# The scan of the source ranking reads its ones from PSUM in place of SBUF

## The reference, cut to what matters

```
edge_index = jnp.stack([src, dst])
...
sums = jnp.zeros((n_entities, res.shape[-1]), res.dtype).at[head].add(res)
counts = jnp.zeros((n_entities,), res.dtype).at[head].add(1.0)
return sums / jnp.clip(counts, 1.0, None)[:, None]
```

## Time and profile before

| | us |
|---|---|
| median of 3 runs | 19270.44 |
| lowest, highest | 19254.84, 19276.73 |
| the profiled execution, timed | 19271.95 |
| its span in the profile | 19270.1 |
| scatter's loop in it: first call to the end of the last call | 542.3 to 2855.0 |
| of it, blocks with `order_node`: first scan to last scan | 1574.3 to 2802.3 |

### The profile page before, as it was taken

The page is one execution under the profiler, slowest core; times in us unless marked ns, Lnnn a source line. Parts: engine busy times, 40 slices in busy tenths (PEclk is TensorE's granted clock), DMA queues, the critical chain, the costliest instruction groups (busy, mean ns, idle before and its releaser), DMA issues. The chain is left out here.

```text
span 19270.1 us, 218526 instructions
## 1 busy us (share of the span) xinstructions
PE 9310.3 (48%) x50893; PEld 6358.9 (33%) x50894; DVE 14747.2 (77%) x25325; ACT 3949.6 (20%) x9903; POOL 12260.2 (64%) x12680
## 2 busy tenths in 40 slices
PE   0343325566666666655777763333243334344343
PEld 0333322232233233222333353333243334334333
DVE  8556668999999999998888832221488888688887
ACT  0111101111111111111000000000144444344443
POOL 0677876666666666663777727777376665566663
PEclk9999996666666666666888855555555655565555
DMA  5333221111111111112222211112532223233223
GB/s 212 76 83 72 69 71 29 25 27 26 25 27 26 25 26 27 25 25 24 29 30 29 28 13 26 26 26 26 66 75 70 73 74 62 69 75 75 68 73 55
DMA packets 1107684, 958.58 MB, mean 50 GB/s; under 512 B 758507, under 2 KB 874859, under 8 KB 1097292
## 3 DMA queue, kind: packets, MB, share of 16 engines
q0 software_dynamic: 368704, 436.55, 12.9%
q1 hardware_dynamic: 738316, 514.36, 10.4%
HBM read 736.74 MB, written 212.93 MB: 49 GB/s over the span
## 5 line engine op out<-in xcount | busy, mean ns | idle before, releaser
L1585 POOL DMA_INDIRECT tail<-ball,h_idx x3328 | 3493.3, 1050 | 2040.4 <-issue 1005.9
L835 PE MATMUL p_rad<-w_stack,hid_t 99*128 99x512 bf16 (+1 forms) x6656 | 2659.1, 551 | 2397.0 <-DVEq L932 1331.9
L905 DVE TENSOR_REDUCE red<-prod 128x96 f32<-128x1536 f32 x1664 | 2901.0, 1743 | 3.5
L1616 PE MATMUL h_sum<-head,h_hot 128*128 128x64 f32 x6656 | 1248.5, 375 | 3164.2 <-ACT head L1671 2993.5
L1616 PEld LDWEIGHTS h_sum<-head,h_hot 128*128 128x128 f32 x6656 | 1220.1, 287 | 3177.0 <-issue 3177.0
L343 POOL DMA_INDIRECT rec_a<-rec,slot x1600 | 1825.3, 1141 | 516.5 <-issue 487.2
L1229 POOL DMA_INDIRECT l_xg<-h_tab,l_idx x1664 | 1570.0, 944 | 835.9 <-issue 500.5
L835 PEld LDWEIGHTS p_rad<-w_stack,hid_t 99*128 99x128 bf16 (+1 forms) x6656 | 716.3, 122 | 4024.7 <-issue 3894.3
L1028 POOL DMA_INDIRECT l_xg<-x_tab,l_idx x1664 | 1570.2, 944 | 658.6 <-issue 493.3
L1042 PE MATMUL l_sum<-outer,l_hot 128*128 128x512 f32 x3328 | 1664.5, 665 | 531.2 <-DVEq L1087 531.2
L752 POOL DMA_INDIRECT l_xg<-in_x,l_idx x1664 | 1577.7, 948 | 522.9 <-issue 475.4
(11 more groups left out here) (408 smaller groups left out, 19410.8 us busy)
## 6 DMA issues: line engine op xcount, KB each, us to landing
hot_t<-rows_l SPq DMA_DIRECT2D x208, 512.0 KB
rec_a<-fill SPq DMA_DIRECT2D x128, 728.0 KB, 19.4
l_rec<-rec_a SPq DMA_DIRECT2D x104, 896.0 KB, 4.8
rhot_t<-rows_r SPq DMA_DIRECT2D x208, 384.0 KB
tail<-ball,h_idx POOLq DMA_INDIRECT x3328, 2.5
t<-in_type SPq DMA_DIRECT2D x100, 512.0 KB
l_xg<-in_x,l_idx POOLq DMA_INDIRECT x1664, 2.4
l_xg<-x_tab,l_idx POOLq DMA_INDIRECT x1664
```

The source lines that it names most:

```text
L835: ins = pe.matmul(p_rad[j % 3][:, h * 512:(h + 1) * 512], hid_t[j // 4 % 2][0:K3 + 3 * (1 - i), j % 4, i, :], w_stack[i][0:K3 + 3 * (1 - i ...
L905: ch.step(dve.tensor_reduce(red[q][:, j, :], prod[j % 3][:, :, :], AX, ALU.add))
L1585: pool.indirect_dma_start(tg[q][:, j, :], None, table[:, :], bass.IndirectOffsetOnAxis(ap=idx[q][:, j:j + 1], axis=0)).then_inc(gathered[q ...
L1616: ins = pe.matmul(p_sum[u % 2][:, j % BT // 2, :], hot[j // HP8 % 3][:, j % HP8, :], hg[:, j, 0:D], start=(j % 2 == 0), stop=(j % 2 == 1))
```

## The change

The first tensor of the scan in `order_node` is `p_row[0:EP, 1:2]`, the column of PSUM that holds 1.0, broadcast to 1600 elements, where it was the SBUF tensor. The result is the same. The scan in `rank_phase` keeps the SBUF tensor, and the tensor stays allocated and filled. No instruction is added, removed or moved on any engine.

```
             def order_node(c):
                 ch.do(dve.tensor_scalar(mask[:, :], high[:, :], g["row"][0:EP, bass.ds(c, 1)], None, ALU.is_equal))
-                ch.do(dve.tensor_tensor_scan(run[:, :], g["ones_et"][:, :], mask[:, :], offs[:, bass.ds(c, 1)], ALU.mult, ALU.add))
+                ch.do(dve.tensor_tensor_scan(run[:, :], p_row[0:EP, 1:2].broadcast_to([EP, ET]), mask[:, :], offs[:, bass.ds(c, 1)], ALU.mult, ALU.add))
                 ch.do(dve.copy_predicated(order[:, :], mask[:, :].bitcast(U32), run[:, :]))
```

## The result

The changed kernel takes 19135.92 us (median of 6 runs, 19124.11 to 19146.55), the kernel before 19260.89 (6 runs, 19254.84 to 19276.73): 125 us less, a ratio of 0.9934 with a 95% interval of 0.9921 to 0.9947. The prediction was 19161, between 19133 and 19208.

What follows compares the result with a forecast made beforehand. GpSimd's calls were taken to pace the blocks that rank by source. Gains of 63.8 us (q = 0) and 45.6 us (q = 1) made 109, so 19270.4 - 109 = 19161 us, range 19133 to 19208.

Steps and rivals of the forecast that it cites:

- What bounds the blocks: In the blocks that rank by source, GpSimd's calls set the pace; VectorE has 7.3 us to spare in each block.
- Kinds of inputs: A GpSimd call starting under a VectorE instruction with two SBUF tensors waits for its end; with one in PSUM it doesn't.
- The first rival: At the source ranking's scan: it holds GpSimd calls as before, whatever its inputs; no change, 19270 us; chance 0.08.
- The scan's own time: The source ranking's scan stays at 3.55 us, 0.02 shorter to 0.1 longer, hidden under VectorE's waiting; worth nothing by itself.
- The walk, q = 0: GpSimd calls at the scan in 25 blocks with q = 0: four done instead of two, 2.55 us each, 63.8 us.
- The walk, q = 1: GpSimd calls at the scan in 24 blocks with q = 1: gain 1.27 or 2.55 us, mean 1.9 taken, 45.6 us.
- the upper bound: Far end of the saving: two GpSimd calls gained in each of 49 source-ranking blocks, 49 × 2.55 = 125 us.
- The first block: First of 50 source-ranking blocks: no gain, since its scan comes behind `place_nodes`, when VectorE is late and isn't waiting.
- The copy: Predicated copy behind the scan takes back part of the gain: with q = 0 it costs a call 1.33 us, before 0.82.

## Why the prediction was right

*What bounds the blocks.* GpSimd's calls, as it said. To do the scan from PSUM twice cost 21 to 33 us of some 180, and to leave it out gained nothing (the calls add 4 us); a second scan from SBUF, which holds a call, cost 106 to 110.

*Kinds of inputs.* The step from three other operations to the scan held: 125 calls start inside the 50 scans of the changed kernel, and the longest of them is like any undisturbed one, 0.97 us. The same broadcast from SBUF freed no call. The first rival, a scan that holds whatever it reads, is out by the result itself.

*The scan's own time.* 3.549 us against 3.551, no change. The fixed part that the Trainium skill ("VectorE: DVE Perf Modes", section on the TRN2 errata) gives a PSUM source, 62 cycles more, isn't seen: the scan is not longer by 0.065 us. That rule gave a sum of 125 us, which is near the result, but not for its reason.

*The walk, q = 0.* Four calls where there were two, as walked through: the calls start 0.30, 1.57, 2.85 and 4.12 us behind the scan's start, and the walk had them at 0.30, 1.58, 2.85 and 4.12.

*The walk, q = 1.* This is the term that was mis-sized. I took 24 × 1.9 = 45.6 us as the mean of one call gained and two; the call starts 0.01 us before the copy and that suffices, so two calls are gained: 24 × 2.55 = 61 us. With it the sum is 63.8 + 61.2 = 125, the upper bound that the prediction named; measured, 125.0 in the medians. That the end that came out was inside the range is the prediction's doing; which end it would be, it could not say.

*The first block.* The prediction gave it no gain, as VectorE is late there, and that was wrong: what counts is that a call is held, not that VectorE waits. Its first scan held a call too, and after the change it doesn't (before, then after):

```profile
1574.33 3.55 DVE L431 TENSOR_TENSOR_SCAN s_run<-ones_et,s_offs,s_mask 128x1600 f32<-128x1600 f32 x1
1575.36 3.31 POOL L343 DMA_INDIRECT rec_a<-rec,slot  x1 [0.30 <-issue]
...
1574.19 3.55 DVE L431 TENSOR_TENSOR_SCAN s_run<-s_row,s_offs,s_mask 128x1600 f32<-128x1600 f32 x1
1575.22 0.96 POOL L343 DMA_INDIRECT rec_a<-rec,slot  x1 [0.30 <-issue]
```

So 50 blocks gained, 50 × 2.55 = 127.5 by the walk and 125.7 at the end of the loop, 2.51 each. The prediction's bound of 125 left this block out; that a block gained 0.04 us less than the walk has it brings the result back to the bound, which is luck.

*The total.* Of the 25 us between 19161 and 19136, the second call in the blocks with q = 1 is 16; the other 9 are that the median of the kernel before came out at 19260.89 with three more runs, in place of 19270.44.

*The other numbers.* The mean call came to 1.117 us (1.13 was predicted), the longest to 2.45 (below 2.9), the wait of L473 to 4.8 (5.1), the last scan's start to 2679.0 (2693).

*The copy.* The prediction said that it would take part of the gain back. With the copy left out its holds come to 49 us, where they were some 40 before.

## What to carry to other kernels

Where GpSimd issues indirect DMAs back to back and sets the pace, look at what VectorE does beside a long call, and not at how long VectorE takes: an input moved from SBUF to PSUM was worth 2.5 us here for an instruction of 3.55 that got no faster, and a comparison in a form that took 1.82 us in place of 1.05 was worth another 0.5 a block. Count what is gained in whole calls, by walking the timeline with the hold taken out, since the next instruction that holds takes a part of it back. Such an edit is free only as long as the other engine waits; two more scans in a block already ate it all.

## What the runs showed of the hardware that was not expected

Holds differ by what holds and by which of the two began first. A call that starts in an instruction with two SBUF tensors, or in a comparison with a scalar that doesn't also count, ends 0.78 to 0.84 us behind it, where nothing else holds it on. A call that began first is not held by the copy, not even with 0.006 us of lead. By a comparison with a scalar it is, if that begins early in the call: in 48 of the 100 blocks before the change the comparison of types begins 0.07 to 0.11 us into a call, and the call ends 0.12 to 0.13 behind it. In 46 others it begins 0.49 to 0.60 us into a call; then the call takes 0.97, and the comparison 1.39 to 1.5 us in place of 1.28. One of each kind after the change: a comparison that begins 0.11 us into a call, and a call that begins under the mask.

```profile
2039.71 1.51 POOL L343 DMA_INDIRECT rec_a<-rec,slot  x1 [0.30 <-DVEq L491]
2039.82 1.28 DVE L469 TENSOR_SCALAR kinds<-t,lane 64x2048 f32<-64x2048 int32 x1 [0.32 <-DVE rec L489]
2041.35 1.05 DVE L430 TENSOR_SCALAR s_mask<-high,row 128x1600 f32<-128x1600 f32 x1 [0.26 <-DVE kinds L469]
2041.52 1.72 POOL L343 DMA_INDIRECT rec_a<-rec,slot  x1 [0.30 <-issue]
```

Chips differ. The kernel before took 19262.8 us in one group, and 24294.76 and 23934.45 in two others. In the changed kernel's profile on one of these the waits from 600 to 1500 us, beside those of the chip of the first kind, are:

```profile
PEld p_all L363 <- issue: 417.7, 243, 7.0
POOL rec_a L343 <- issue: 350.4, 549, 11.2
...
PEld p_all L363 <- issue: 140.5, 43, 3.7
POOL rec_a L343 <- issue: 196.3, 644, 0.3
```

TensorE waits 243 times where it waited 43, in the middle of its matmuls and for nothing that the profile names, and GpSimd rests up to 11.2 us before a call. What it lacked isn't shown by any run. The change's gain was there all the same: 139 us, a ratio of 0.9952 where it is 0.9934 on the other chip.
